# Two on-chip recurrences: states, step weights and pre-states lie on partitions 96 to 127 instead of 0 to 31

## What is computed

```
def step(state, u_t):                   # L0: state is 16 sequences x 16 numbers
    state = jnp.tanh(state @ A.T + u_t)
    return (state, state)
...
_, states = jax.lax.scan(step, init, u_tm)
y = jnp.einsum('bls,es->ble', states, Cm) + z * D
```

## Time and profile before

| what | value |
|---|---|
| median of 3 runs | 777.11 us (775.06 to 777.71) |
| span of the profiled execution | 775.8 us |
| what lies around the span, median less span | 1.3 us |
| instructions | 10987 |
| busy share: TensorE, VectorE, ScalarE | 73%, 44%, 43% |
| granted TensorE clock, mean | 0.763 of full |

### The profile page before, as it was taken

How to read it: one execution, slowest core, us unless ns; L and a number is a source line. 1 busy time by engine, 2 the same in 40 slices (tenths; PEclk the granted TensorE clock), 3 DMA queues, 4 the chain that set the end, 5 groups by cost and what they waited for, 6 DMA issues and landing times. The chain is left out here.

```text
span 775.8 us, 10987 instructions
## 1 busy us (share of the span) xinstructions
PE 566.2 (73%) x4080; PEld 324.7 (42%) x4081; DVE 340.6 (44%) x734; ACT 336.1 (43%) x1095; POOL 0.2 (0%) x4
## 2 busy tenths in 40 slices
PE   6665566567877999986566666665899998995463
PEld 5322222235645766664333333333455544551321
DVE  2170000049757788875200000006887546776233
ACT  2233333337737677772333333334544465442121
POOL 0000000000000000000000000000000000000000
PEclk9755555559997999997555555558999999997577
DMA  4000000000000000000000000004000000000000
GB/s 166 1 1 1 1 0 1 1 0 1 3 0 1 2 1 2 2 1 1 1 1 1 0 1 1 0 1 108 1 2 1 1 1 1 2 1 0 8 5 27
DMA packets 4954, 6.73 MB, mean 9 GB/s; under 512 B 1186, under 2 KB 4642, under 8 KB 4772
## 3 DMA queue, kind: packets, MB, share of 16 engines
q1 hardware_dynamic: 4900, 6.01, 2.5%
HBM read 3.38 MB, written 0.52 MB: 5 GB/s over the span
## 5 line engine op out<-in xcount | busy, mean ns | idle before, releaser
L303 PE MATMUL ps<-arena,wsb 16*16 16x16 f32 (+1 forms) x1024 | 131.5, 206 | 111.1 <-ACT arena L321 111.1
L321 ACT ACTIVATE arena<-ps 16x16 f32<-16x16 f32 (+1 forms) x512 | 96.3, 188 | 199.3 <-PE ps L303 199.3
L303 PEld LDWEIGHTS ps<-arena,wsb 16*16 16x16 f32 (+1 forms) x1024 | 76.4, 118 | 196.2 <-ACT arena L321 191.7
L327 DVE TENSOR_TENSOR X<-X,ps 128x128 f32<-128x128 f32 x16 | 4.6, 288 | 206.6 <-PE ps L288 206.6
L965 ACT ACTIVATE arena<-ps 128x512 f32<-128x512 f32 x96 | 56.6, 597 | 62.0 <-PE ps L726 60.7
L1267 DVE TENSOR_TENSOR arena<-arena,ps 128x512 f32<-128x512 f32 x96 | 64.0, 685 | 41.2 <-ACT arena L965 24.9
L744 PE MATMUL ps<-arena 128*32 128x128 f32 x768 | 60.3, 279 | 7.3 <-DVE arena L1267 7.3
L889 ACT ACTIVATE arena<-ps,arena 128x128 f32<-128x128 f32 (+1 forms) x128 | 52.4, 418 | 29.9 <-DVE arena L1140 29.8
L744 PEld LDWEIGHTS ps<-arena 128*32 128x32 f32 x768 | 34.8, 109 | 41.9 <-DVE arena L1267 22.6
L1139 DVE TENSOR_REDUCE arena<-ps 128x2 f32<-128x512 f32 (+1 forms) x48 | 33.0, 688 | 18.6 <-PE ps L569 11.1
L586 PE MATMUL ps<-wsb,arena 128*128 128x128 f32 x192 | 30.4, 282 | 11.6 <-DVE arena L1148 11.5
(11 more groups left out here) (231 smaller groups left out, 805.8 us busy)
## 6 DMA issues: line engine op xcount, KB each, us to landing
arena<-xn SPq DMA_DIRECT2D x16, 128.0 KB, 2.5
wsb<-weights SPq DMA_DIRECT2D x1, 1916.5 KB, 8.8
wsb<-weights SPq DMA_DIRECT2D x1, 549.5 KB, 4.8
X<-x SPq DMA_DIRECT2D x1, 512.0 KB, 3.9
out<-X SPq DMA_DIRECT2D x1, 512.0 KB, 3.0
csb<-consts SPq DMA_DIRECT2D x1, 160.0 KB, 8.8
arena<-w SPq DMA_DIRECT2D x2, 64.0 KB
arena<-b SPq DMA_DIRECT2D x4, 0.5 KB
```

Of the source, the lines that this page charges most:

```text
L303: nc.tensor.matmul(step_columns(k, rows, r), w_state, states[0:rows, :, :, t].rearrange("p g j -> p (g j)"), start=False, stop=True, skip_ ...
L321: nc.scalar.activation(states[0:rows, :, :, t + 1].rearrange("p g j -> p (g j)"), step_columns(t // STEP_BANK, rows, t % STEP_BANK), func) ...
```

## The change

Two constants, STATE_ROWS and STEP_ROWS, both 96, are added to the first partition of all that belongs to a step. Nothing is added or removed; the instructions, their order, their sizes and their semaphores stay.

```diff
+STATE_ROWS = 96
+STEP_ROWS = 96
...
         def bank_fill(n, k, g, rows, w_in):
-            mm = nc.tensor.matmul(ps[0:rows, k, g * P:(g + 1) * P], w_in[:, C * g:C * g + rows],
+            mm = nc.tensor.matmul(ps[STEP_ROWS:STEP_ROWS + rows, k, g * P:(g + 1) * P], w_in[:, C * g:C * g + rows],
...
         def bank_out(k, g, rows, w_out):
-            mm = nc.tensor.matmul(ps[C * g:C * g + C, k, 0:P], w_out, states[0:rows, g, :, STEP_BANK * k + 1:STEP_BANK * (k + 1) + 1],
+            mm = nc.tensor.matmul(ps[C * g:C * g + C, k, 0:P], w_out, states[STATE_ROWS:STATE_ROWS + rows, g, :, STEP_BANK * k + 1:STEP_BANK * (k + 1) + 1],
...
         def step_columns(k, rows, t):
-            return ps[0:rows, k, :].rearrange("p (b t) -> p b t", t=STEP_BANK)[:, :, t]
+            return ps[STEP_ROWS:STEP_ROWS + rows, k, :].rearrange("p (b t) -> p b t", t=STEP_BANK)[:, :, t]
...
-                nc.tensor.matmul(step_columns(k, rows, r), w_state, states[0:rows, :, :, t].rearrange("p g j -> p (g j)"),
+                nc.tensor.matmul(step_columns(k, rows, r), w_state, states[STATE_ROWS:STATE_ROWS + rows, :, :, t].rearrange("p g j -> p (g j)"),
...
-                nc.scalar.activation(states[0:rows, :, :, t + 1].rearrange("p g j -> p (g j)"),
+                nc.scalar.activation(states[STATE_ROWS:STATE_ROWS + rows, :, :, t + 1].rearrange("p g j -> p (g j)"),
...
-            recur_tensor(pe, 0, NS, u_w[:], W("L0_AT", NS)[:, 0:NS], g1[0:NS, 0:C])
+            low = STATE_ROWS
+            recur_tensor(pe, 0, NS, u_w[:], W("L0_AT")[low:low + NS, low:low + NS], g1[low:low + NS, low:low + C])
...
-            recur_tensor(pe, 1, C, W("ident"), W("F_VT", C)[:, 0:C], W("ident", C)[:, 0:C])
+            recur_tensor(pe, 1, C, W("ident"), W("F_VT")[low:low + C, low:low + C], W("ident")[low:low + C, low:low + C])
...
-                nc.vector.tensor_scalar(ps[0:NS, k, :], ps[0:NS, k, :], u_b[0:NS], None, ALU.add).then_inc(s["bank biased"], 1)
+                bank = ps[STEP_ROWS:STEP_ROWS + NS, k, :]
+                nc.vector.tensor_scalar(bank, bank, u_b[STEP_ROWS:STEP_ROWS + NS], None, ALU.add).then_inc(s["bank biased"], 1)
```

## The result

The changed kernel is slower: 780.33 us median (779.62 to 784.69, 9 runs) against 777.11 (772.89 to 778.2, 9 runs), a ratio of 1.0069 with a 95% interval of 1.0044 to 1.0093. The ratio is taken over all runs; the two medians alone would give 1.0041. The profiled execution has a span of 780.2 us instead of 775.8.

What follows compares the result with a forecast made beforehand. The prediction held the kernel bound by the latency of two TensorE-ScalarE loops. Its terms, all 0, left the span at 775.8 us; with 1.3 us around it the median was 777.1 us, range 768.5 to 781.

Steps and rivals of the forecast that it cites:

- The loop bounds it, and only latency counts there: Both recurrences: a closed loop of TensorE and ScalarE, 512 turns, 284 of 775.8 us, paced by latency, not throughput.
- The activation: I take 0, ends -4 and +4 ns: The step's activation on lanes 96 up: costs the same as at lane 0, within 2 us either way.
- The matmul: I take 0: The step's matmul on rows and columns 96 up: no change, ends -17 and +5 ns a step (-8.7 and +2.6 us).
- clock comparison: Steps at 2.4 against 1.2 GHz, 500 and 509 ns: a shorter way through the array saves at most 17 ns.
- rival A: Step matmul: results leave the last block sooner, saving mostly near 8 ns a step, 773.0 us, 768.4 at best; chance 0.30.
- B: Step matmul: the whole way through the array is saved, 80 ns a step, 41 us, so 736 us; chance 0.05.
- Every ns of a turn is 0.51 us: Both recurrences: each ns a turn gets shorter or longer counts 512 times, as nothing else can run instead.
- The rest, some 490 us, must not move at all: Everything outside the two loops keeps its time; a difference there would make the forecast wrong.
- Rival C: Step matmul: the last row block gets data later, 5 ns a step, 779.7 us, or 781.7 with the activation; chance 0.22.
- bias_bank, bank_out and bank_fill at nothing: Instructions around the steps: moving them costs 0; the 56 turns lengthened by bank_fill, 0.2 us each, stay.

## Why the prediction was right or wrong

It was wrong: I forecast no change that can be told, and the kernel is slower by 0.69%. The median lies inside the range, near its upper end, and slower had a chance of 0.22. That the median is inside the range is in part luck: the loops, which the range was made for, give 2.3 us, and the rest of what was lost comes from a cause that the prediction doesn't have.

- *The loop bounds it, and only latency counts there*: right. The two loops are the places that changed by themselves.
- *The activation: I take 0, ends -4 and +4 ns*: this step failed first. I compared activations by how many lanes they reach, and no row had one that started elsewhere, nor did I price PSUM and SBUF apart. The runs show +5 ns for reading PSUM on partitions 96 up and -2 ns for writing SBUF there. The sum, +3 ns, was inside my ends; the zero rested on rows that say nothing of where a lane starts. The loops' 2.3 us are just what the prediction held to be the least that a measurement can tell.
- *The matmul: I take 0*: inside its ends, but not 0 for certain; the part from the weight load to the activation grew by 1 to 3 ns. The steps of the changed kernel got no shorter, so the clock comparison's bound of 17 ns wasn't put to a test, and rival A's and B's shorter way through the array did not show. By that, the Trainium skill's sentence in "TensorE: Matmul & The Clock Gate", "Step-by-step: what each phase is for", on 128 cycles down the rows gives nothing that a kernel could save by choosing rows 96 up: with the states alone moved, plain turns stayed at 507 and 560 ns.
- *Every ns of a turn is 0.51 us*: failed in the second loop, whose turns come in lengths of 560 or 567 ns. There the 3 ns of the activation, with up to 3 ns in the matmul's part, became nearly 7 in 227 turns, which is 1.5 us in that loop against the second profile of the kernel before. In the first loop a plain turn grew by 4.1 ns. Turns that come in steps also weaken the prediction's clock comparison: its 500 and 509 ns may lie a step apart whatever the latency did.
- *The rest, some 490 us, must not move at all*: failed, and it is the larger half. Of the 4.9 us between the mean spans (779.7 and 774.8), the loops hold 2.3 and all that lies outside them about 2.5; in the profiled pair that is 4.5 us more behind the loops and 2.3 less ahead of them. I had read the clock row only to see that the loops are slow, not to ask what a later end of them does to the stages behind.
- *Rival C*: right in sign and near in size (it asked for 4.6 ns a turn; plain turns grew by 4.1 ns in the first loop and 6.2 in the second), wrong in place. It put the delay into the array's last block of rows. With the rows alone moved no turn got longer; the cost sits on the pre-state's side, and with that side alone moved 5 ns of it are in the activation, which reads PSUM there.
- *bias_bank, bank_out and bank_fill at nothing*: right. Turns with a bank_fill stayed at 780 ns in the second loop and near 700 in the first, those with a bank_out were like the plain ones.

Not tried: PSUM read and matmul output apart from each other, since the activation must read where the matmul writes.

## What to carry to other kernels

In a closed loop between two engines, measure a turn in ns and count the lengths that occur: in one of the two loops here a few ns of latency cost a whole step of 7 ns, in the other about what they were. Keep the PSUM side of such a loop on the first partitions; 32 or 64 cost nearly as much here as 96. When a change moves the time of a stage by a us or two, look at the granted clock in the stages behind it before calling the remainder noise, and lengthen the loop by other means to tell the two apart. Compare what lies ahead of the change as well: here it took 21.7 to 26.6 us in the profiled executions.

## What the runs showed of the hardware that was not expected

- A [16 or 32] x 16 activation took 188 ns with both sides on partition 0 up, 189 with both on 32 or 64 up, 191 with both on 96 up, 193 with PSUM alone and 186 to 187 with SBUF alone on 96 up.
- The second loop's plain turns took 560 or 567 ns and almost nothing between; the first loop's lay from 505 to 517 ns, most of them near 507 or 513, with no such gap.
- A loop of 135 us that ended 0.99 us later cost the stretch behind it 2.1 us more at a clock that fell back twice; with 3.5 us more in the same loop that stretch took 207.3 us, as before.
- The 16 matmuls of line 240 ahead of the first loop took 421 ns at the median in one profiled execution and 275 in another, whose step 0 started at 21.7 instead of 26.35 us.
